# Seven-product gate and up projections of the shared expert, begun one batch earlier

## The reference, cut to what matters

```python
gs = jnp.einsum('th,fih->tfi', x, sh_gate_w)          # 4096 x 512 times 512 x 1024
us = jnp.einsum('th,fih->tfi', x, sh_up_w)            # the same size
y_sh = jnp.einsum('tfi,fhi->tfh', jax.nn.silu(gs) * us, sh_down_w)
out = out + jnp.einsum('tf,tfh->th', global_w[:, E_DYN:], y_sh)
```

## Time and profile before

| | |
|---|---|
| three runs | 1254.98, 1261.3 and 1262.98 us; median 1261.3 |
| profiled execution | 1259.68 us, its span 1257.9 us, granted clock 0.991 on average |
| PE busy | 1204.5 us, 96% of the span |
| DVE busy | 952.3 us, 76% |
| ACT busy | 709.4 us, 56% |
| POOL busy | 582.2 us, 46% |

### The profile page before, as it was taken

How to read it: one execution, slowest core, us unless ns; L and a number is a source line. 1 busy time by engine, 2 the same in 40 slices (tenths; PEclk the granted TensorE clock), 3 DMA queues, 4 the chain that set the end, 5 groups by cost and what they waited for, 6 DMA issues and landing times.

```text
span 1257.9 us, 29768 instructions
## 1 busy us (share of the span) xinstructions
PE 1204.5 (96%) x10916; PEld 838.5 (67%) x10916; DVE 952.3 (76%) x2006; ACT 709.4 (56%) x1988; POOL 582.2 (46%) x685
## 2 busy tenths in 40 slices
PE   6888998889999999999999999999999999999996
PEld 3555655678888888886444444777777777666663
DVE  5899898799999998887677777777777775645451
ACT  4377787699999998896344222222222231555553
POOL 0047678537667776732300000777776100355624
PEclk9999999899999999999999999999999999999999
DMA  9522023133545454553890051222223510687846
GB/s 346 210 68 69 1 33 45 43 94 131 169 144 173 161 162 149 165 165 115 169 209 1 10 159 34 69 35 69 48 55 87 200 68 1 218 174 204 188 55 84
DMA packets 132224, 144.01 MB, mean 114 GB/s; under 512 B 53200, under 2 KB 86128, under 8 KB 132080
## 3 DMA queue, kind: packets, MB, share of 16 engines
q1 hardware_dynamic: 114240, 119.65, 32.1%
q0 software_dynamic: 13248, 21.15, 9.3%
q10 hardware_dynamic: 4592, 1.32, 0.5%
HBM read 84.93 MB, written 57.19 MB: 113 GB/s over the span
## 4 chain that ended last, share of the span: by engine, by line
PE 86%; DVE 7%; issue 2%; DMA 2%; ACT 2%; POOL 1%; SPq 0%; DVEq 0%; POOLq 0%; ACTq 0%
PE bank L121 31%; PE bank L2126 15%; PE bank L2119 13%; PE bank L1503 6%; PE bank L1435 4%; PE bank L955 4%; PE bank L1456 3%; PE bank L1450 3%; PE bank L1421 2%; PE bank L1024 2%; PE bank L2405 1%; PE bank L872 1%; DMA q_rows<-att_land 1%; PE bank L961 1%; PE bank L891 1%
## 5 line engine op out<-in xcount | busy, mean ns | idle before, releaser
L1624 POOL DMA_INDIRECT lists<-att_land x128 | 133.1, 1040 | 208.8 <-DVE att_land L1764 167.4
L1353 ACT ACTIVATE att_land<-bank,att_land 128x120 f32<-128x120 f32 x512 | 178.3, 375 | 15.5 <-DVE att_land L1221 15.4
L2119 PE MATMUL bank<-att_land 128*128 128x512 f16 x768 | 176.2, 379 | 0.6 <-DVE program_logits L1304 0.6
L1946 ACT ACTIVATE att_land<-program_x 128x512 f32<-128x512 f32 x40 | 25.2, 631 | 195.1 <-DVE program_x L2088 195.1
L2119 PEld LDWEIGHTS bank<-att_land 128*128 128x128 f16 x768 | 75.0, 98 | 82.1 <-issue 0.6
L121 PE MATMUL bank<-program_xs,program_wgu 128*128 128x512 f16 x576 | 128.7, 379 | 0.6 <-DVE att_land L1723 0.6
L121 PE MATMUL bank<-att_land 128*128 128x128 f16 (+2 forms) x1944 | 113.5, 212 | 1.0 <-issue 0.5
L1353 ACT ACTIVATION_READ_ACCUMULATOR att_land<-bank,att_land 128x1 f32 x512 | 112.9, 221 | 0.0
L121 PEld LDWEIGHTS bank<-att_land 128*128 128x128 f16 x1944 | 105.3, 98 | 5.9 <-issue 1.3
L1785 POOL DMA_INDIRECT att_land<-xn_rows,att_land x40 | 39.1, 978 | 143.2 <-DMA out_rows<-att_land 98.9
L121 PEld LDWEIGHTS bank<-program_xs,program_wgu 128*128 128x128 f16 x576 | 56.2, 98 | 67.6 <-DVE att_land L1723 1.1
(11 more groups left out here) (299 smaller groups left out, 2827.2 us busy)
## 6 DMA issues: line engine op xcount, KB each, us to landing
att_land<-q_rows SPq DMA_DIRECT2D x96, 128.0 KB, 2.6
xn_rows<-att_land SPq DMA_DIRECT2D x37, 256.0 KB, 3.9
out_rows<-att_land SPq DMA_DIRECT2D x37, 256.0 KB, 2.5
q_rows<-att_land SPq DMA_DIRECT2D x32, 256.0 KB, 2.9
xt_tiles<-att_land SPq DMA_DIRECT2D x32, 256.0 KB, 2.1
x_rows<-program_x SPq DMA_DIRECT2D x8, 1024.0 KB, 4.6
att_land<-x_rows SPq DMA_DIRECT2D x8, 1024.0 KB, 5.8
program_xs<-xt_tiles SPq DMA_DIRECT2D x28, 256.0 KB, 5.0
```

Source lines behind the costliest of these rows:

```text
L1353: last = act.activation(prob[:, c, h, :], ps_s[c % 2][:, h, :], ACT.Exp, bias=nmax[:, u % 2, c, h:h + 1], accum_out=rsum[:, u % 2, n:n + 1])
L1624: pool.indirect_dma_start(out=io["lists"], out_offset=bass.IndirectOffsetOnAxis(ap=index[:, t, k:k + 1], axis=0), in_=load[:, t, k, :], in ...
L2119: last = pe.matmul(ps_y[i][:, :], hid[:, c % 2, a, i * P:(i + 1) * P], wd[:, q, c, :], start=c == 0 and n == 0, stop=c == NC - 1 and n == 2)
```

## The change

The plain form ends after two batches instead of three. The sums of the weights move from units 9 to 20 into units 3 to 14. The sums of the first batch of tokens move from units 20 to 23 (for batch 3) into units 13 to 15 (for batch 2). The router's last five pieces are now in block-product units (16, 18, 20, 22 and 24), in the middle of the unit, behind the DVE operation on line 2073 and the token sums. The output rows of batch 1 are no longer scaled in one go in unit 17; the block-product loop scales them in two pairs in the same unit, as it does for the later batches. The arithmetic of each block product is as before.

```diff
-    SEVEN = 3 * NC
-    SUMS_AT = {9: 0, 11: 1, 13: 2, 15: 3, 16: 4, 17: 5, 18: 6, 19: 7}
-    TOK_AT = 20
+    FROM = 2
+    SEVEN = FROM * NC
+    SUMS_AT = {3: 0, 5: 1, 7: 2, 8: 3, 9: 4, 10: 5, 11: 6, 13: 7}
+    TOK_AT = 13
+    LATER = (16, 18, 20, 22, 24)
...
         def token_high(b, j):
-            need(act, s["tok_new"], 14 * (b - 2) + 7 * j + 6)
+            need(act, s["tok_new"], 14 * (b + 1 - FROM) + 7 * j + 6)
...
         def token_sums(b):
-            chained = [14 * (b - 3)]
+            chained = [14 * (b - FROM)]
...
-                need(dve, s["tok_hi"], 2 * (b - 3) + j + 1)
+                need(dve, s["tok_hi"], 2 * (b - FROM) + j + 1)
...
-            if v == 2 * NC + 1:
-                rows(1, range(TB))
             if v - 1 in SUMS_AT:
                 next(begun)
             if v in SUMS_AT:
                 begun = weight_sums(SUMS_AT[v])
                 next(begun)
-            if SHIFT <= v < 2 * NC - 1 or v in (2 * NC, 18, 20, 22, 23):
+            if SHIFT <= v < 2 * NC - 1:
                 next(pieces)
...
+            if v in LATER:
+                next(pieces)
             if c == 1:
                 rows(b - 1, range(2))
...
-                need(pe, s["tok_new"], 14 * (b - 2))
+                need(pe, s["tok_new"], 14 * (b + 1 - FROM))
```

## The result

The changed kernel takes 1299.3 us (median of four runs, 1297.4 to 1303.4), the kernel before 1259.9 beside it; the ratio is 1.032, with a 95% interval of 1.030 to 1.034. The forecast was 1302 in a range from 1286 to 1311. The profiled execution took 1303.4 us, 43.7 more than that of before.

A forecast was written before the change was run, and what follows sets the result against it. PE was taken to bound the kernel before, DVE the changed one up to unit 16. The sum -4.6 + 41.9 + 2.0 + 2.4 = +41.7 on 1259.7 us gave 1301.4, written as 1302, range 1286 to 1311.

The forecast's parts named there:

- What bounds: Shared expert: PE bounds the kernel before; once changed, DVE's own time is the path from unit 6 to unit 16.
- Block products, -4.6: Units 16 to 23: block products take 57.52 us instead of 62.16, a gain of 4.6 us of PE time.
- The loads, 19.3: Unit 3: DVE's first weight sum waits 19.3 us, until 651.8, for the fp32 weight loads.
- Weight sums, tokens and ACT, 13.6 + 9.1 + 4.4: DVE up to unit 16: added weight sums 13.6 us, batch 2 token sums 9.1, delays by ACT's rounding 4.4.
- the 85.2 us: DVE's time from unit 3's `hf` to unit 16's, if never waited upon: 95.6 us less 10.4 of slack.
- The path of PE's halts: PE stands some 15 us ahead of up of unit 6, and again until about 761 us before unit 16.
- Restart, +2.0: After the halt before unit 16, PE runs about 4 us at the lower clock, costing 2.0 us (0 to 4).
- Pieces, +2.4: Units 18 and 22: router pieces joined with token sums hold up PE, costing 2.4 us (0 to 5).
- The lists: POOL's chain: lists come one unit later plus the whole delay, covered by 78 us, so no cost.
- Vector load without the weights' wait: Rival, unit 3: loads end early enough, the 19.3 us drop out, 1282 us; chance 0.06.
- The other side: Rival, unit 6 and first block product: DVE's lag absorbs everything added, only -4.6 is left, 1255 us; chance 0.04.
- PE too slow as well: Rival, DVE-bound stretch: PE's waits drop it to 1.2 GHz, six relapses of 2 us, 1314 us; chance 0.07.

The follow-up runs named there:

- e9: The changed kernel run once more, with no edit, for the length of DVE's wait at the loads: 1299.8 us, ratio 1.031 to the kernel before.
- e1: The changed kernel with the eight weight sums begun in units 6 to 13 instead of 3 to 13: 1278.3 us, ratio 1.015.
- e3: The changed kernel with a semaphore of its own for the first fp32 weight load, the only one the first sum waits for: 1287.8 us, ratio 1.023.
- e8: e1 with batch 2's token sums left out and zeros filled in by GpSimd, so its output rows are wrong: 1269.9 us, ratio 1.008.
- e7: The same step half as far: block products from unit 20 on, weight sums begun in units 8 to 18, later token sums: ratio 1.0065.
- e4: The changed kernel with the router's last five pieces in units 16, 20, 24, 28 and 32: 1297.8 us, ratio 1.030.
- e6: e5 with the router's last five pieces in units 16, 20, 24, 28 and 32: 1447.9 us, ratio 1.004.
- e10: The kernel before with 42 unused GpSimd operations (two fills, 40 additions) added beside DVE's router pieces: ratio 1.002.
- e5: The changed kernel with the four sums of each weight chunk and batch 2's token sums moved from DVE to GpSimd: ratio 1.007.

## Why the prediction was right

*What bounds.* That PE hands over to DVE in this stretch is shown by e9's table, where the wait moves the first block product one for one, and by e1, e3 and e8, each of which took away a wait or work of DVE's and moved the time by about that much.

*Block products, -4.6.* From the first block product of unit 16 to that of unit 24 lie 62.1 us (763.15 to 825.22). Less 1.64 of slow matmuls and 2.72 of halts these are 57.7, against the 57.5 taken. By the estimate from the figures in the Trainium skill, "TensorE: Matmul & The Clock Gate", "Back-to-back issue gap", this would have been a loss; the rows here speak against it as those of before did.

*The loads, 19.3.* 21.5, 18.5 and 17.5 us in three traces of this order. The wait changes from run to run by 2 us either way, so that the value came so close to the mean of them is in part luck; e1 without it is 21 us faster.

*Weight sums, tokens and ACT, 13.6 + 9.1 + 4.4.* From `hf` of unit 3 (630.65) to the last token sum (763.05) DVE took 132.4 us, against 131.6 in the sum. Taking out the wait, 110.9 against 112.3: the sum was 1.4 us too large, and the term that was mis-sized is ACT's. The eight second parts and the four rows of eight first parts in the trace have the counts and durations of the working:

```profile
L2013 DVE SCALAR_TENSOR_TENSOR program_x<-att_land,program_x 128x1024 f16<-128x1024 f32 x8 | 9.8, 1220 | 0.0
L1959 DVE TENSOR_TENSOR att_land<-att_land 128x512 f16<-128x512 f32 x12 | 8.3, 693 | 11.2 <-ACT att_land L1899 11.2
...
L2006 DVE TENSOR_TENSOR att_land<-program_x 128x256 f32<-128x256 f32 x8 | 3.4, 423 | 21.6 <-DMA program_x<-in_sh_guT 21.5
```

These are DVE's groups by line, 655 to 764 us. The low parts waited 11.2 us for 12, 0.93 each, and the earlier trace rows had 17.7 for 13: the slack of before has been used, as the 85.2 us assumed. What is left over 0.70 each, 2.8 us, is ACT's delay, which the prediction had at 4.4. DVE waited for PE nowhere between the loads and the first block product, as forecast. In e1 the same sum holds within 3 us: 109.7 us against 112.3, with 1.7 for ACT. It fails in e7, where DVE was not behind all the way: there the last token sum ended 130.7 us after `hf` of unit 3, where my working gives 122.8.

*The path of PE's halts.* I had named two halts; there are four: 17.7 us in unit 6, 6.3 in unit 10 (ACT's copy of batch 0), 2.8 in unit 13 (the router's count) and 10.1 at unit 16. They sum to 37.0. The rest of the 43.6 is some 6 us of matmuls at 1.2 GHz (behind the halts of 17.7, 6.3 and 2.8 us the row that follows each is 2.6, 1.7 and 1.8 us longer than its like) and 0.9 us by which the whole stage began later. The total was right all the same, because DVE's work set it and PE's halts only divide it up.

*Restart, +2.0.* The 24 matmuls took 4.26 for 2.62: 1.6 us.

*Pieces, +2.4.* 1.43 and 1.29, and e4 removes them: 2.7 us.

*The lists.* POOL's scatter began at 832.7 instead of 786.4 (885.8 in e4), and PE waited for no gathered row in either.

The sum was +41.7; the profiled execution has +43.7 and the medians +39.4, with the wait at the loads as the largest part that changes between them. Against the profiled execution the loads were 2.2 us too small, ACT's part 1.5 too large, and the stage began 0.9 later: errors that partly cancel.

*The rivals.* "Vector load without the weights' wait", 1282, is what e1 makes of the kernel (1278). The other side, 1255, failed at the two places named: unit 6 and the first block product. "PE too slow as well" did not come: PE's slow matmuls were some 6 us ahead of unit 16, and DVE's own 110.9 us were the longer way all the same.

## What to carry to other kernels

A step that gives an engine less to do pays only if what feeds it can be there earlier. Ask of each moved operation when its data lands, and what is queued behind its wait on an in-order engine: here one wait for loads that three units later would have cost nothing was half of the loss. Slack on the engine that takes the moved work is spent unit by unit and can't be saved for a deadline; add up its work up to the deadline, with the waits that it would have when it isn't behind. And before work is moved to an idle engine, look what the two do to each other: additions on GpSimd doubled many of DVE's operations.

## What the runs showed of the hardware

GpSimd's additions lengthened DVE's two-input operations from 0.42 to as much as 0.94 us, and one of 128x32 from 0.19 to 1.03 (e6, e10). Of the one-input ones a reduction (0.42) and a reciprocal (0.35) were not touched; the scalar operation on line 1683 was (0.29 to 0.70, e10), and a copy of 128x32 stood for 3.25 us instead of 0.18 until GpSimd's fill was over (e8). I had counted GpSimd as free help.

In the runs of e5, e6 and e7 the kernel before took 1441 to 1442 us instead of 1258 to 1261, and the three kernels beside it as much more. It is not a matter of one chip: the record has e5 and e6 on chip 12 and e7 on chip 4, and on chip 12 again, in e10, the kernel before took 1258.8. Up to the router's scatter the three traces run as elsewhere; then, while POOL scatters and just behind it, PE and DVE halt again and again for 14 to 38 us, with no releaser that belongs to the kernel. The halts move with the scatter: it begins at 798.7 in e5 and at 850.2 in e6, and the first long halt of PE ends at 860.6 and at 911.4. PE's timeline of e5, with DVE's row for the same time:

```profile
860.13 0.42 DVE L2115 TENSOR_TENSOR program_x<-bank,program_x 128x256 f32<-128x256 f32 x1 [35.08 <-DMA program_x<-in_L_WqT]
860.61 1.46 PE L2158 MATMUL bank<-program_xs,program_wgu 128*128 128x256 f16 x6 [35.37 <-issue]
```

The DMA named there belongs to a load that was over long before. What it is stays open; it wasn't tried. It is why their times are compared only with the kernel before as it ran beside them.
